# Delta rule in one Trainium2 program: key-query and key-key products merged into one 256-column matmul, decay rows from one 512-column matmul

## Chip, cores and metric

One NeuronCore of one Trainium2 (trn2) chip runs the whole program. The metric is the device time of one execution in microseconds, as the median of several runs; lower is better. TensorE's clock has two levels here, 2.4 and 1.2 GHz, and the profile prints the granted level as 1.00 and 0.50, or a mean between them.

## The reference

The program is four transformer-like layers on an array of shape (8, 512, 128). The change touches only the attention of the last layer, a gated delta rule with 8 heads, key size 128 and value size 32:

```python
def step(state, inp):
    q_t, k_t, v_t, a_t, b_t = inp
    retained = jnp.einsum('bhvk,bhk->bhv', state, k_t)
    rk = retained[..., None] * k_t[:, :, None, :]
    vk = v_t[..., None] * k_t[:, :, None, :]
    state = a4 * (state - b4 * rk) + b4 * vk
    o_t = jnp.einsum('bhvk,bhk->bhv', state, q_t)
    return (state, o_t)
```

Here `a_t = exp(g)` is the decay and `b_t` the write strength. q, k and v come from a projection, a causal convolution of four taps and silu; the output is normalised, gated and projected.

## The kernel before

The recurrence over 512 positions is done in four chunks of 128 positions. Eight heads are split into two groups of four. A *unit* of work is one group of one batch row: its four chunks are inverted and solved, and beside that the data of the next unit (taps, norms, gates, keys) are prepared. The loop body `delta_units` holds two units, called a and b below, and runs 7 times; `delta_first` and `delta_second` come ahead of it, `delta_last` behind it. I write a0 to a3 and b0 to b3 for the four chunk periods of units a and b in the loop body.

Each chunk period has nine turns, 0 to 8, and every engine's program is written out by `in_turn` in the same order of turns. In chunk period i three things go on at once:

- `solve` of chunk i-1 (turn 0 "state": products with the state S; then four small triangular steps; turn 8 "finish": output and new state),
- `make` of chunk i+1 in three parts (turns 0, 3 and 6),
- `invert` of chunk i (32x32 block products, one per turn),

and then the pieces of `prepare` that `pieces(u)` sets for this turn. In some turns there are none; of these, the prediction names turn 6 of a3, b0, b1 and b3 (b0 has only a ScalarE piece there), where TensorE has nothing from `prepare`.

The parts of `make`, with the lines of the kernel before:

- Part 0. TensorE writes the running sum of the decay along the rows into bank 1 (`mk`): four matmuls of 128 columns, one a head (L1725). VectorE subtracts and clips it into `D` (L2013), ScalarE takes the exponential (L1928), POOL masks it with `upto3` (L1893).
- Part 1. TensorE makes the key-query products of four heads in bank 1 (L1733, `kq`); VectorE multiplies them with `D` into `P` (L2018).
- Part 2. TensorE makes the key-key products in the same bank (L1733 again, `kk`), after `P` was read; VectorE scales `D` by `gam` (L2023) and multiplies into `A` (L2026); ScalarE copies A's diagonal blocks (L1932); POOL makes `M` from them (L1898).

A float32 matmul appears in the trace as two records, so four matmuls are "x8". `solve` uses banks 2 and 7 in turn, one for even and one for odd chunks. Its "state" step waits on TensorE for `S` and for the output of the chunk two before (`outs`), then runs L1778; VectorE's side reads the bank at L2059 and L2060, computes `r` (L2062, L2067), copies `W` (L2070), and at turns 7 and 8 makes `zz` and `ze` (L2073, L2076), then `S` (L2087), `o1` (L2088) and `O` (L2090). TensorE's "finish" is L1796 and L1803. The inverse is L1740 on TensorE, L1938 on ScalarE and L2039 with the transpose L2041 on VectorE. POOL also squares q and k for their norms (L1918, waits for ScalarE's silu L1962), copies the input (L1905) and weights the gates (L1910). The taps are L1841, the squares' sums L1849, the norm's second matmul L1817.

## Time and profile before

| | |
|---|---|
| median of 3 runs | 4906.73 us (4898.85 to 4908.08) |
| the profiled execution, its own time | 4906.74 us |
| its span, first to last instruction | 4904.7 us |
| mean granted clock of TensorE over the span | 0.779 |
| TensorE matmul, weight load, VectorE, ScalarE, POOL busy | 81%, 52%, 49%, 31%, 15% |
| delta rule, 2925 to 4790 us of the span | TensorE busy 1707.31 of 1865.00 us |

The profile is of one execution. It gives busy time by engine, strips over 40 slices of the span, groups of instructions by line with the idle time ahead of them, and, for any stretch, the instructions in order of time. Idle time of an engine counts only where the engine sets the pace.

### The profile page before, as it was taken

The numbers are of one execution on the slowest core, as the hardware profiler recorded it, in microseconds if no ns is written. First come the engines' busy times: TensorE is split into PE (matmuls) and PEld (weight loads), VectorE is DVE, ScalarE is ACT, GpSimd is POOL, SyncE is SP. The second block draws the span as 40 slices with busy tenths as digits, with TensorE's granted clock in tenths as the row PEclk, the third lists the DMA queues.
The fourth block names the chain that finished last, engine by engine and source line by source line (L and its number), as shares of the span: only waits on it lengthen the run. The fifth ranks groups of instructions, "written<-read, shape, count | busy, mean of one in ns | idle before, by whom it ended". The sixth has DMA issues, their size and how long they took to land. (4 is left out here: it accounts for less than half of the span.)

```text
span 4904.7 us, 125869 instructions
## 1 busy us (share of the span) xinstructions
PE 3978.9 (81%) x55640; PEld 2529.9 (52%) x55640; DVE 2418.5 (49%) x6071; ACT 1503.3 (31%) x2781; POOL 747.0 (15%) x741
## 2 busy tenths in 40 slices
PE   3557776999858787878787868999898989999985
PEld 1225663444335555555554324666666666666671
DVE  3556775233277777777771112444344443434444
ACT  2443233455422222222212322322232222223223
POOL 1112221000021212111110002211111212111111
PEclk8776667999865556655557979898898889888967
DMA  2000000422000000000000010000000000000000
GB/s 73 0 0 1 0 0 6 64 35 35 15 2 3 3 3 3 3 3 3 3 3 14 0 53 1 2 2 2 2 2 2 2 2 2 2 2 2 2 2 19
DMA packets 18964, 45.89 MB, mean 9 GB/s; under 512 B 4864, under 2 KB 8320, under 8 KB 17408
## 3 DMA queue, kind: packets, MB, share of 16 engines
q1 hardware_dynamic: 18432, 37.95, 3.3%
q8 instruction: 438, 7.18, 0.6%
q14 instruction: 94, 0.77, 0.1%
HBM read 35.71 MB, written 2.23 MB: 8 GB/s over the span
## 5 line engine op out<-in xcount | busy, mean ns | idle before, releaser
L1841 PE MATMUL ps<-d_hp,d_w_qk 128*128 128x512 f32 x1024 | 520.0, 632 | 8.0 <-ACT d_QK L1962 8.0
L1031 PE MATMUL ps<-g_Q,g_K 32*32 32x32 f32 (+1 forms) x12288 | 275.7, 246 | 28.5 <-issue 12.9
L1841 PEld LDWEIGHTS ps<-d_hp,d_w_qk 128*128 128x128 f32 x1024 | 179.3, 194 | 226.2 <-issue 201.0
L1031 PEld LDWEIGHTS ps<-g_Q,g_K 32*32 32x32 f32 x12288 | 238.0, 134 | 73.7 <-PE ps L1031 39.3
L852 PE MATMUL ps<-ex_hs,w_c_fc 128*128 128x512 f32 x512 | 232.7, 598 | 20.1 <-DVE ex_hs L818 20.1
L1938 ACT ACTIVATE d_F<-ps 128x128 f32<-128x128 f32 x256 | 70.8, 277 | 520.1 <-PE ps L1740 519.7
L863 PE MATMUL ps<-ex_r,w_c_proj 128*128 128x512 f32 x512 | 230.0, 592 | 0.0
L1063 PE MATMUL ps<-g_S,g_V 32*64 32x32 f32 x4096 | 160.6, 287 | 79.7 <-DVE g_H L1239 60.5
L826 DVE TENSOR_TENSOR ex_r<-ex_r 128x512 f32<-128x512 f32 x128 | 88.5, 692 | 277.2 <-ACT ex_r L840 277.2
L840 ACT ACTIVATE ex_r<-ps 128x512 f32<-128x512 f32 x256 | 151.5, 592 | 236.4 <-PE ps L852 236.3
L2070 DVE COPY d_W<-ps 32x128 f32<-32x128 f32 x256 | 73.0, 285 | 277.6 <-PE ps L1790 275.5
L1898 POOL TENSOR_TENSOR d_M<-d_A,w_joins 128x128 f32<-128x128 f32 (+1 forms) x128 | 112.0, 896 | 588.0 <-ACT d_A L1932 588.0
L1918 POOL TENSOR_TENSOR d_sq<-d_QK 128x512 f32<-128x512 f32 x128 | 133.1, 1042 | 402.4 <-ACT d_QK L1962 353.2
L1063 PEld LDWEIGHTS ps<-g_S,g_V 32*64 32x64 f32 x4096 | 127.4, 203 | 128.9 <-DVE g_H L1239 69.1
L2067 DVE TENSOR_TENSOR d_r<-d_r,ps 32x128 f32<-32x128 f32 x192 | 55.0, 287 | 264.0 <-PE ps L1783 247.9
L1047 PE MATMUL ps<-g_V,g_KT 32*32 32x64 f32 x4096 | 154.2, 286 | 25.0 <-issue 5.3
L1928 ACT ACTIVATE d_D<-d_D 128x512 f32<-128x512 f32 x64 | 40.3, 629 | 434.3 <-DVE d_D L2013 434.2
L852 PEld LDWEIGHTS ps<-ex_hs,w_c_fc 128*128 128x128 f32 x512 | 98.1, 192 | 144.1 <-issue 123.4
L1778 PE MATMUL ps<-d_S,d_QK 128*128 128x32 f32 x768 | 137.1, 345 | 36.2 <-issue 32.5
L1733 PE MATMUL ps<-d_QK 128*128 128x128 f32 x1024 | 162.0, 306 | 0.8 <-DVE d_P L2018 0.8
L1740 PE MATMUL ps<-d_X,d_M 32*32 32x32 f32 x8192 | 129.7, 199 | 38.4 <-DVE d_X L2036 24.5
L1893 POOL TENSOR_TENSOR d_D<-d_D,w_upto 128x512 f32<-128x512 f32 x64 | 85.5, 1335 | 492.4 <-ACT d_D L1928 492.4
(464 smaller groups left out, 8263.6 us busy)
## 6 DMA issues: line engine op xcount, KB each, us to landing
ex_root<-gate_rows SPq DMA_DIRECT2D x8, 2048.0 KB, 15.4
d_QK<-in_conv_qk_dram SPq DMA_DIRECT2D x2, 2048.0 KB, 7.4
X<-in_x_dram SPq DMA_DIRECT2D x1, 2048.0 KB, 11.4
w_c_fc<-in_c_fc_dram SPq DMA_DIRECT2D x1, 2048.0 KB, 7.7
w_c_proj<-in_c_proj_dram SPq DMA_DIRECT2D x1, 2048.0 KB, 12.1
out_dram<-X SPq DMA_DIRECT2D x1, 2048.0 KB, 6.3
w_wmod<-in_wmod_dram SPq DMA_DIRECT2D x1, 1536.0 KB, 6.8
w_w<-in_w_dram SPq DMA_DIRECT2D x2, 768.0 KB, 5.3
```

The costliest lines, as they stand in the source:

```text
L840: e.activation(r[:, n % 2, f], hidden(f), ACT.Relu).then_inc(act.steps, act.did(f"r{n}{f}"))
L852: e.matmul(hidden(f), k.w["c_fc"][:, n % E, ts(f, C)], hs[:, n % 3], start=True, stop=True).then_inc(pe.steps, pe.did(f"u{n}{f}"))
L863: e.matmul(total(b), k.w["c_proj"][:, x, f, :], r[:, n % 2, f], start=(x == 0 and f == 0), stop=(x == E - 1 and f == F - 1)).then_inc(pe.s ...
L1031: ins = e.matmul(later(scored, n_), keys_, queries(n_, planes, r, 4 * i + j), start=(turn_ == 0 and part == 0 and n_ != 1), stop=(part == ...
L1047: ins = e.matmul(P[2 * odd + 1][ts(h4, 32), 256 + j * 64:320 + j * 64], KT[rows, (KR, KI)[part], i, ts(h4, 32)], V[rows, i, 4 * sg + h4, ( ...
L1063: ins = e.matmul(P[4 + bank][ts(second, 64), t], V[rows, i, 4 * sg + h4, (slice(32, 96), slice(0, 64))[part]], S[rows, i % 2, h4, part, :] ...
L1733: ins = e.matmul(mk[:, ts(h, C)], QK[:, 1, H, t], QK[:, part - 1, H, t], start=True, stop=True)
L1740: ins = e.matmul(inv[rows, h], stationary[rows, h], moving[rows, h], start=True, stop=True, tile_position=(32 * j, 32 * j))
L1778: ins = e.matmul(b[:, half * 128 + 32 * h:half * 128 + 32 * h + 32], QK[:, what, H, ts(c, C)], S[:, H], start=True, stop=True)
L1841: ins = e.matmul(b, w_qk[:, j, c, ts(H, C)], hp[:, j:j + T], start=(j == 0), stop=(j == TAPS - 1))
L1898: e.tensor_tensor(M[:, a, levels], A32[:, a].unsqueeze(1).to_broadcast([C, many, 4, 32]), k.w["joins"][:, levels].unsqueeze(2).to_broadcas ...
L1918: e.tensor_tensor(squares(x), qk, qk, ALU.mult).then_inc(pool.steps, pool.did(f"{tag}sq{x}"))
```

## The change

The two groups of products of a chunk become one: for each head one matmul with the key as stationary side and query and key together as 256 moving columns. Their results need two banks: heads 0 and 1 in bank 1, heads 2 and 3 in bank 7. So `solve` has bank 2 alone, and its "state" step waits for the output of the chunk just before. The decay's rows come from one matmul of 512 columns with `ones3` as stationary side, over a product of `upto3` and `g` that POOL writes into `D` (new part 3 of `make`). VectorE reads the two banks in two instructions for `P` and two for `A`, each of 256 columns.

```diff
-        bank = lambda i: P[(2, 7)[i % 2]]
+        pair = [P[x].rearrange("p (h w x) -> p w h x", h=2, w=2) for x in (1, 7)]
+        bank = lambda i: P[2]
         MAKE = {0: 0, 3: 1, 6: 2}
+        MAKE_SECOND = {0: 3, 2: 0, 4: 1, 6: 2}
+        EARLY = NI - 1
...
+                            if t == 3 * NI - 1:
+                                make(u, NT, 3)
...
-                            if turn in MAKE and (i + 1 < NT or u["next"]):
-                                make(u, i + 1, MAKE[turn])
+                            parts = MAKE if i else MAKE_SECOND
+                            if turn in parts and (i + 1 < NT or u["next"]):
+                                make(u, i + 1, parts[turn])
                             invert(u, i, step, l)
                             for piece in at[NI * i + turn]:
                                 prepare(u, *piece)
+                            if turn == EARLY and (i + 2 < NT or i + 2 == NT and u["next"]):
+                                make(u, i + 2, 3)
... tensor engine
-                            for h in range(4):
-                                ins = e.matmul(mk[:, ts(h, C)], q["g"][:, c, 4 * g + h:4 * g + h + 1].to_broadcast([C, C]), k.w["upto3"][:], start=True, stop=True)
-                            ins.then_inc(pe.steps, pe.did(f"gb{n}"))
+                            e.wait_ge(pool.steps, pool.at(f"u{n}"))
+                            e.matmul(mk, k.w["ones3"][:], f2(D[:, g]), start=True, stop=True).then_inc(pe.steps, pe.did(f"gb{n}"))
...
-                            e.wait_ge(dve.steps, dve.at((f"d{n}", f"P{n}")[part - 1]))
+                            e.wait_ge(dve.steps, dve.at(f"d{n}"))
                             for h in range(4):
                                 H = 4 * g + h
-                                ins = e.matmul(mk[:, ts(h, C)], QK[:, 1, H, t], QK[:, part - 1, H, t], start=True, stop=True)
-                            ins.then_inc(pe.steps, pe.did((f"kq{n}", f"kk{n}")[part - 1]))
+                                ins = e.matmul(pair[h // 2][:, :, h % 2], QK[:, 1, H, t], QK[:, :, H, t], start=True, stop=True)
+                            ins.then_inc(pe.steps, pe.did(f"kk{n}"))
...
-                            if c % 2 in outs:
-                                e.wait_ge(dve.steps, dve.at(f"out{outs[c % 2]}"))
-                            outs[c % 2] = n
+                            if outs:
+                                e.wait_ge(dve.steps, dve.at(f"out{outs[-1]}"))
+                            outs.append(n)
... gpsimd
+                        if part == 3:
+                            if i == NT:
+                                e.wait_ge(dve.steps, dve.at(u["tag"] + "g"))
+                            if made:
+                                e.wait_ge(dve.steps, dve.at(f"A{made[-1]}"))
+                            made.append(n)
+                            e.tensor_tensor(D[:, g], k.w["upto3"][:].unsqueeze(1).to_broadcast([C, 4, C]),
+                                            q["g"][:, c, 4 * g:4 * g + 4].unsqueeze(2).to_broadcast([C, 4, C]), ALU.mult).then_inc(pool.steps, pool.did(f"u{n}"))
... vector engine
-                            e.tensor_tensor(Pm[:, a], v4(mk), D[:, g], ALU.mult).then_inc(dve.steps, dve.did(f"P{n}"))
+                            for x in range(2):
+                                e.tensor_tensor(Pm[:, a, ts(x, 2)], pair[x][:, 0], D[:, g, ts(x, 2)], ALU.mult).then_inc(dve.steps, dve.did(f"P{n}"))
...
-                            e.wait_ge(pe.steps, pe.at(f"kk{n}"))
                             e.wait_ge(dve.steps, dve.at(f"dg{n}"))
-                            e.tensor_tensor(A[:, a], v4(mk), D[:, g], ALU.mult).then_inc(dve.steps, dve.did(f"A{n}"))
+                            for x in range(2):
+                                e.tensor_tensor(A[:, a, ts(x, 2)], pair[x][:, 1], D[:, g, ts(x, 2)], ALU.mult).then_inc(dve.steps, dve.did(f"A{n}"))
```

The first place is TensorE in a0, from the second state-solving step to the start of a1. Before, in program order:

```order
L1790 MATMUL ps<-d_r,d_Y 32x32 x4
L1733 MATMUL ps<-d_QK 128x128 x4
L1740 MATMUL ps<-d_X,d_M 32x32 x16
L1817 MATMUL ps<-d_sq,w_mean 128x512
L1783 MATMUL ps<-d_W,d_A 32x32 x4
L1740 MATMUL ps<-d_F,d_Y 32x32 x16
L1868 MATMUL ps<-w_ident,d_QK 128x128 x4
L1790 MATMUL ps<-d_r,d_Y 32x32 x4
L1740 MATMUL ps<-d_X,d_M 32x32 x16
L1783 MATMUL ps<-d_W,d_A 32x32 x4
L1733 MATMUL ps<-d_QK 128x128 x4
L1740 MATMUL ps<-d_F,d_Y 32x32 x16
```

And of the change, the same stretch (its lines carry other numbers: L1795 is L1790 of before, L1745 is L1740, L1818 or L1822 the norm, L1788 is L1783, L1873 is L1868):

```order
L1795 MATMUL ps<-d_r,d_Y 32x32 x4
L1745 MATMUL ps<-d_X,d_M 32x32 x16
L1822 MATMUL ps<-d_sq,w_mean 128x512
L1788 MATMUL ps<-d_W,d_A 32x32 x4
L1738 MATMUL ps<-d_QK 128x256 x4
L1745 MATMUL ps<-d_F,d_Y 32x32 x16
L1873 MATMUL ps<-w_ident,d_QK 128x128 x4
L1795 MATMUL ps<-d_r,d_Y 32x32 x4
L1745 MATMUL ps<-d_X,d_M 32x32 x16
L1788 MATMUL ps<-d_W,d_A 32x32 x4
L1745 MATMUL ps<-d_F,d_Y 32x32 x16
```

The products of turn 3 are now at turn 4 (only in the first chunk period of a unit; else they stay at turn 3) and twice as wide, and nothing stands any more between L1783's and L1740's successors at turn 6.

The second place is POOL in a0 and the start of a1. Before, from the loop's start:

```order
L1893 TENSOR_TENSOR d_D<-d_D,w_upto 128x512
L1905 ISA
L1905 COPY d_xb<-X 128x512
L1898 TENSOR_TENSOR d_M<-d_A,w_joins 128x128
L1898 TENSOR_TENSOR d_M<-d_A,w_joins 128x512
L1910 TENSOR_TENSOR d_values_gates<-d_values_gates,w_o_norm_w 128x4x128
L1918 TENSOR_TENSOR d_sq<-d_QK 128x512
L1893 TENSOR_TENSOR d_D<-d_D,w_upto 128x512
```

And of the change:

```order
L1904 TENSOR_TENSOR d_D<-w_upto,d_g 128x512
L1920 ISA
L1920 COPY d_xb<-X 128x512
L1908 TENSOR_TENSOR d_D<-d_D,w_upto 128x512
L1913 TENSOR_TENSOR d_M<-d_A,w_joins 128x128
L1913 TENSOR_TENSOR d_M<-d_A,w_joins 128x512
L1925 TENSOR_TENSOR d_values_gates<-d_values_gates,w_o_norm_w 128x4x128
L1933 TENSOR_TENSOR d_sq<-d_QK 128x512
L1904 TENSOR_TENSOR d_D<-w_upto,d_g 128x512
L1908 TENSOR_TENSOR d_D<-d_D,w_upto 128x512
```

L1904 is the new product, once at the very start and once for chunk 2; the second stands behind the first square of q and k (L1933, before L1918), and TensorE's decay matmul of a1 (L1731) waits for it.

The third place is ScalarE at the start of unit a. Before:

```order
L1928 ACTIVATE d_D<-d_D 128x512
L1938 ACTIVATE d_F<-ps 128x128
L1948 ACTIVATE d_sq<-ps 128x512
L1958 ACT_TABLE_LOAD
L1958 ACTIVATE d_values_gates<-ps 128x2x128 x3
L1938 ACTIVATE d_F<-ps 128x128
```

And of the change:

```order
L1953 ACTIVATE d_F<-ps 128x128
L1963 ACTIVATE d_sq<-ps 128x512
L1973 ACT_TABLE_LOAD
L1973 ACTIVATE d_values_gates<-ps 128x2x128 x2
L1943 ACT_TABLE_LOAD
L1943 ACTIVATE d_D<-d_D 128x512
L1973 ACT_TABLE_LOAD
L1973 ACTIVATE d_values_gates<-ps 128x2x128
L1953 ACTIVATE d_F<-ps 128x128
```

The exponential of `D` now stands between silus, with a table load on either side of it.

## Rows read from the trace of the kernel before

**Rows 1.** The page: busy time, share of the span and count, by engine.

```profile
PE 3978.9 (81%) x55640; PEld 2529.9 (52%) x55640; DVE 2418.5 (49%) x6071; ACT 1503.3 (31%) x2781; POOL 747.0 (15%) x741
```

**Rows 2.** Windows: busy time by engine in one loop iteration and one calm stretch.

```profile
core 0: us, PE busy (x) PEld busy (x) DVE busy (x) ACT busy (x) POOL busy (x), PEclk, DMA share, GB/s
3319.00:3551.00 232.00, 213.96 (x3220) 147.65 (x3221) 95.30 (x295) 64.64 (x150) 44.17 (x43) 0.88 0.01 2
3398.00:3430.30 32.30, 30.51 (x500) 25.87 (x501) 13.80 (x48) 7.32 (x21) 5.66 (x6) 0.75 0.01 2
```

**Rows 3.** Timeline (start, duration, engine, line) of TensorE: two taps, then the next group.

```profile
3349.61 1.96 PE L1841 MATMUL ps<-d_hp,d_w_qk 128*128 128x512 f32 x4
3351.50 0.43 PE L1790 MATMUL ps<-d_r,d_Y 32*32 32x32 f32 x8
```

**Rows 4.** Timeline of turn 6 and 7 in b1, TensorE and VectorE.

```profile
3484.96 1.16 PE L1733 MATMUL ps<-d_QK 128*128 128x128 f32 x8
3485.39 0.69 DVE L2023 TENSOR_TENSOR d_D<-d_D,d_gam 128x512 f32<-128x512 f32 x1
...
3486.05 0.45 PE L1740 MATMUL ps<-d_F,d_Y 32*32 32x32 f32 x32
3486.19 0.69 DVE L2026 TENSOR_TENSOR d_A<-ps,d_D 128x512 f32<-128x512 f32 x1
...
3486.34 0.41 PE L1790 MATMUL ps<-d_r,d_Y 32*32 32x32 f32 x8
3486.79 0.28 DVE L2039 TENSOR_TENSOR d_X<-d_X,ps 128x128 f32<-128x128 f32 x1
...
3487.12 0.45 PE L1740 MATMUL ps<-d_X,d_M 32*32 32x32 f32 x32 [0.37 <-DVE d_X L2039]
```

**Rows 5.** Timeline of the key-query products in a3, at the lower clock.

```profile
3414.09 2.08 PE L1733 MATMUL ps<-d_QK 128*128 128x128 f32 x8
```

**Rows 6.** Timeline from turn 7 of a0 to turn 0 of a1, all engines.

```profile
3342.95 1.68 POOL L1898 TENSOR_TENSOR d_M<-d_A,w_joins 128x128 f32<-128x128 f32 x2 [14.70 <-ACT d_A L1932]
...
3343.61 1.17 DVE L2073 TENSOR_TENSOR d_zz<-d_W,d_gam 128x128 f32<-128x128 f32 x1
...
3344.70 1.75 DVE L2108 TENSOR_TENSOR d_values_gates<-d_values_gates,d_kn 128x512 f32<-128x512 f32 x1
...
3348.36 1.05 PE L1725 MATMUL ps<-w_upto,d_g 128*128 128x128 f32 x8
...
3349.42 0.60 ACT L1962 ACTIVATE d_QK<-ps 128x512 f32<-128x512 f32 x1
...
3350.09 1.04 POOL L1918 TENSOR_TENSOR d_sq<-d_QK 128x512 f32<-128x512 f32 x1 [4.19 <-ACT d_QK L1962]
```

**Rows 7.** The same place in the last of the 7 iterations, TensorE and POOL.

```profile
4497.82 1.05 PE L1725 MATMUL ps<-w_upto,d_g 128*128 128x128 f32 x8
```

```profile
4499.55 1.04 POOL L1918 TENSOR_TENSOR d_sq<-d_QK 128x512 f32<-128x512 f32 x1 [4.19 <-ACT d_QK L1962]
```

**Rows 8.** Timeline of the end of b2: POOL, VectorE, TensorE.

```profile
3516.29 1.67 POOL L1898 TENSOR_TENSOR d_M<-d_A,w_joins 128x128 f32<-128x128 f32 x2 [5.68 <-ACT d_A L1932]
...
3517.05 1.06 DVE L2073 TENSOR_TENSOR d_zz<-d_W,d_gam 128x128 f32<-128x128 f32 x1
...
3518.15 1.01 DVE L2076 TENSOR_TENSOR d_ze<-d_zz,d_end 128x128 f32<-128x128 f32 x1
...
3519.21 0.52 PE L1796 MATMUL ps<-d_zz,d_P 128*128 128x32 f32 x3 [2.27 <-DVE d_ze L2076]
```

**Rows 9.** Windows around two idle places of TensorE: columns as in rows 2.

```profile
3516.40:3519.80 3.40, 1.13 (x46) 1.01 (x44) 2.37 (x3) 2.05 (x3) 2.61 (x3) 1.00 0.02 5
3519.80:3530.00 10.20, 10.20 (x75) 8.92 (x74) 3.02 (x13) 0.00 (x0) 0.00 (x0) 0.50 0.00 0
3461.80:3465.20 3.40, 1.91 (x50) 1.67 (x49) 2.28 (x7) 0.64 (x2) 0.48 (x1) 1.00 0.00 0
3465.20:3468.60 3.40, 3.40 (x4) 0.89 (x4) 2.25 (x8) 1.03 (x6) 1.17 (x1) 0.50 0.00 0
```

**Rows 10.** Timeline at the end of unit a.

```profile
3425.46 1.06 PE L1778 MATMUL ps<-d_S,d_QK 128*128 128x32 f32 x4
3425.50 0.29 DVE L2090 TENSOR_TENSOR d_O<-d_o,d_qn 128x128 f32<-128x128 f32 x1
```

**Rows 11.** The page's groups: POOL's masking of `D`.

```profile
L1893 POOL TENSOR_TENSOR d_D<-d_D,w_upto 128x512 f32<-128x512 f32 x64 | 85.5, 1335 | 492.4 <-ACT d_D L1928 492.4
```

15 lines of the change are left out of this document (7 added, 8 removed).

## Prediction

> **What bounds the kernel now.** I read the page's busy shares first: TensorE is busy 81% of the span, VectorE 49%, POOL 15% [rows 1]. Then the windows by stage: in one iteration of the delta loop TensorE works 213.96 of 232.00 us at a mean clock of 0.88 [rows 2]. So here TensorE's queue sets the pace; a microsecond counts when it lengthens that queue, opens a gap in it, or turns the clock down. The chain that ended last lies in the last layers and says nothing of this stage, so I read the timeline of one iteration engine by engine instead. The reader should see two kinds of place: turns in which TensorE has taps or sums behind the small steps and never waits, and turns without them, where it waits for VectorE (0.37 us in [rows 4]). An iteration comes 7 times; I cost one iteration and multiply. The profiled execution took 4906.74 us with a span of 4904.7, the same as the median of the runs to 0.01 us.
>
> **The products.** Four heads of 128 columns take 1.09 us from their start to the next group's (3484.96 to 3486.05, [rows 4]). Two taps of 512 columns take 1.89 us (3349.61 to 3351.50, [rows 3]), 0.945 each, against 0.27 for one head. No row has 256 columns. Between the two, 0.27 + (0.945 - 0.27)/3 = 0.495 a head, so 1.98 us for four; since the 0.27 holds the start of a group I take 1.95. The bounds are 1.09 (columns free) and 2.18 (nothing saved). The two old groups took 2.18, so a chunk saves 0.23 us of TensorE's work. The decay's rows went from four matmuls of 128 columns to one of 512: 0.945 against about 0.98 to 1.09, nothing.
>
> The Trainium skill ("TensorE: Matmul & The Clock Gate", section "Wait — 56ns, not 53.3ns?") gives a fixed cost of about 2.5 ns a matmul beside its columns. By that page eight records fewer are an estimated 0.02 us a chunk in place of 0.23, which would add 0.2 us to each chunk's term; the rows above show more than that, since a group's start is in them.
>
> **Where the products stand.** This matters more than their sum. All of the work is now at turn 3 (4 in a0 and b0), 0.86 us longer than before, and 1.09 us are gone from turn 6. In [rows 4], turn 6 without a piece, VectorE goes from `D` times `gam` (3485.39, 0.69) to `A` (3486.19, 0.69) to the subtraction of X (3486.79 to 3487.07), and TensorE's next step waits for that. With the key-key products gone, `A` could start 0.1 us earlier and is two instructions in place of one, which I bound by one more start, about 0.1: the subtraction ends when it did. TensorE comes there 1.09 us earlier and waits 1.09 us longer. These periods (a3, b0, b1, b3) keep the 0.86 us of turn 3 and get nothing back. In a3 and b3 the products run at the lower clock, 2.08 in place of 1.16 us [rows 5], so 0.86 becomes 1.54. Together 2 x 0.86 + 2 x 1.54 = **+4.8 us**. a1 has sums and a tap at turn 6 and saves its 0.23: **-0.2**. In a2 TensorE waits at "finish" anyway, so of 1.09 I give back a third: **+0.5**.
>
> In b2 "finish" waits 2.27 us for `ze`: `zz` takes 1.06 us beside POOL's M and `ze` 1.01 beside a square [rows 8], where a free one takes about the 0.28 of the X subtraction [rows 4]. If `W` comes up to 1.09 us earlier, `zz` starts at 3515.96, ahead of M at 3516.29, and at least 1.1 us of the wait go; if `ze` slips in too, 2.7 go. Net of 0.86 that is -0.2 to -1.8; I take **-0.5**.
>
> **POOL's new product.** It is priced by the masking of the same size, 1.3 us [rows 11]. In most periods POOL is done with it before TensorE asks. At a1 it isn't: it stands behind the first square, which waits for ScalarE's silu (3349.42) and ends at 3351.13; the product would end at 3352.4, while TensorE's decay matmul started at 3348.36 [rows 6]: 4.0 us late. In the last iteration it is the same, 4499.55 + 1.04 + 1.3 against 4497.82 [rows 7], and all seven lie at 4.0. Queued behind the waiting matmul are the gates' sums and the next tap; nothing else can go on. The lower bound: turn 6 is shorter, so `zz` might start ahead of M and not take 1.17, nor `values` 1.75 beside POOL [rows 6]; that brings the silu up to 2.9 us forward and leaves 1.1. I take **+3.1**, nearer to the row. The rule behind the 1.17 and 1.75 is in the Trainium skill ("SBUF — State Buffer", section "Who interferes with whom"): a VectorE instruction with two SBUF inputs is shut out while a GpSimd instruction reads SBUF; by that rule, the trace agrees.
>
> **The clock.** Where TensorE idled 2.27 us of 3.40 the next 10.20 us ran at 0.50; where it idled 1.49 the next 3.40 did [rows 9]. So the wait at a1 (over 3 us for TensorE) should be followed by at least 3.4 us at half speed, in which the work of 1.7 us is lost: **+1.7** (0 to 5.1).
>
> **Small ones.** With one bank for `solve`, "state" waits for `O`. Everywhere but at the end of unit a there is work between; there it started at 3425.46 and `O` ended at 3425.79 [rows 10]: **+0.4**. The table loads around the exponential (two more in a0) fall while ScalarE is mostly free; in b0 the silu that frees a bank comes later: **+0.3**, were that cover gone 1.3 each. Weight loads fall from eight to four heads' worth and lie under matmuls.
>
> **Sum.** 4.8 - 0.2 + 0.5 - 0.5 + 3.1 + 1.7 + 0.4 + 0.3 = 10.1 us an iteration, 71 us for seven. Outside the loop are eight more periods, in which turn 6 is mostly bare: 8 x 0.6 = 5. That is +76 on a span of 4904.7, and 4906.7 + 76 = **4983 us**.
>
> **Rivals.**
> - *The product isn't late* (18%). If the earlier `zz` pulls the silu forward, the term falls to 1.1 and the clock stays up: 10.1 - 2.0 - 1.7 = 6.4 an iteration, 4957 us. For it speaks that 1.09 us earlier is enough in [rows 6] to pass M; against it, that the norm ahead of it sets this point too.
> - *Faster through the clock* (10%). Around a3 and around b3 the clock has a mean of 0.75 over 32.30 us [rows 2]: half of the time at half speed, so 8 us of work are lost at each, 113 us in all. A denser, wider stream of products could hold the higher level. It decides from 76/113, two thirds of that, on; were all of it won, the time would be 4870. Against it: turn 6 becomes emptier at the same place.
> - *Nothing comes of it* (6%): VectorE and TensorE regain in the busy periods what the bare turns lose, since all the waits there are under 0.4 us; 4905.
> - *The clock falls at the bare turns too* (8%): their wait grows to 1.46 us, like the 1.49 of [rows 9]. Four times 1.7 us and seven iterations are 48 more: 5031.
> - The forecast, slower as summed: 58%, its own range 4960 to 5015.
>
> **How the numbers follow.** The range 4925 to 5030 takes in the first rival, the lower bounds of the products and of the wait (4.0 to 1.1), and the last rival's edge; outside are the two that end at or below 4905. Two tenths of a per cent, about 10 us, is what a measurement can tell from no change. Faster 0.10, same 0.06, slower 0.84.
>
> **What would show it.** In the trace of the change: the group of 256 columns at 1.95 us start to next start; an idle of some 1.4 us ahead of the first inverse product of turn 7 in b1, released by VectorE's X; ahead of the decay matmul of a1 an idle of 2 to 4 us released by POOL, and a window at 0.50 behind it; an iteration of 242 us in place of 232. The prediction is wrong if the iteration's mean clock rises above 0.90, if the wait for POOL's product is missing, or if turn 6 turns out to be covered.

## The result, and the profile of the change

The change made the kernel slower: 5026.84 us (median of 4 runs, 5022.06 to 5038.62) against 4906.83 us for the kernel before on the same chip, a ratio of 1.0252 with a 95% interval of 1.0231 to 1.0273. The forecast said 4983 us, with 4960 to 5015 as its own range and 4925 to 5030 as the range over all rivals. Direction and mechanism of most terms hold, the size does not: 120 us in place of 76. The profiled execution took 5038.62 us, span 5036.9 us. It is the slowest of the four, 12 us above the median, so what is read from its trace per iteration of the loop is somewhat high, by some 1.7 us if all of the 12 us lie there (12 / 7).

The page's busy time of the changed kernel, which answers to [rows 1]:

```profile
PE 4052.0 (80%) x54744; PEld 2497.7 (50%) x54744; DVE 2421.7 (48%) x6199; ACT 1521.4 (30%) x2795; POOL 812.9 (16%) x805
```

896 TensorE records fewer, yet 73 us more busy. The windows of the changed kernel: the loop iteration that answers to the first line of [rows 2], then the wait at a1 and the stretch behind it.

```profile
core 0: us, PE busy (x) PEld busy (x) DVE busy (x) ACT busy (x) POOL busy (x), PEclk, DMA share, GB/s
3338.08:3585.72 247.64, 221.07 (x3105) 140.67 (x3105) 97.01 (x311) 67.11 (x152) 52.46 (x51) 0.85 0.01 2
3368.00:3371.10 3.10, 0.04 (x1) 0.07 (x1) 0.00 (x0) 2.08 (x3) 2.04 (x2) 1.00 0.00 0
3371.10:3376.00 4.90, 4.90 (x12) 2.20 (x13) 3.41 (x9) 0.63 (x1) 1.65 (x1) 0.65 0.02 3
```

The mean clock of the iteration went from 0.88 to 0.85: that is where the part of the loss that the forecast lacks will turn out to be. First the places that the prediction named. The timeline of the changed kernel at a1, ScalarE, POOL and TensorE:

```profile
3368.21 0.60 ACT L1977 ACTIVATE d_QK<-ps 128x512 f32<-128x512 f32 x1
...
3368.88 1.04 POOL L1933 TENSOR_TENSOR d_sq<-d_QK 128x512 f32<-128x512 f32 x1 [4.20 <-ACT d_QK L1977]
3369.88 1.04 POOL L1904 TENSOR_TENSOR d_D<-w_upto,d_g 128x512 f32<-128x512 f32 x1
...
3371.06 1.10 PE L1731 MATMUL ps<-d_D,w_ones 128*128 128x512 f32 x2 [4.02 <-POOL d_D L1904]
...
3372.57 3.44 PE L1846 MATMUL ps<-d_hp,d_w_qk 128*128 128x512 f32 x4
```

POOL's product is queued behind the square, which waits for the silu; TensorE idles 4.02 us for it, and the next two taps take 3.44 us in place of the 1.98 that a pair takes at the full clock. This iteration is the exception: in the six others the same wait is 2.46 to 2.53 us. Turns 3, 6 and 7 of b1, TensorE and VectorE, which answer to [rows 4]:

```profile
3505.60 1.99 PE L1738 MATMUL ps<-d_QK 128*128 128x256 f32 x8
3507.53 0.45 PE L1745 MATMUL ps<-d_X,d_M 32*32 32x32 f32 x32
...
3519.24 0.43 PE L1795 MATMUL ps<-d_r,d_Y 32*32 32x32 f32 x8
...
3520.62 0.28 DVE L2055 TENSOR_TENSOR d_X<-d_X,ps 128x128 f32<-128x128 f32 x1
...
3520.95 0.45 PE L1745 MATMUL ps<-d_X,d_M 32*32 32x32 f32 x32 [1.27 <-DVE d_X L2055]
```

The wide group takes 1.93 us to the next start, and at the bare turn 6 TensorE waits 1.27 us for VectorE, where it waited 0.37.

TensorE's waits over the seven iterations, the changed kernel first, then the kernel before. Columns: engine and line that waits, what ended it, us in total, times, the longest.

```profile
PE ps L1783 <- issue: 32.7, 6, 6.9
PE ps L1745 <- DVE d_X L2055: 31.4, 28, 1.3
PE ps L1801 <- DVE d_ze L2092: 29.5, 31, 2.3
PE ps L1745 <- DVE d_X L2052: 20.5, 16, 1.5
PE ps L1731 <- POOL d_D L1904: 19.0, 7, 4.0
```

```profile
PE ps L1778 <- issue: 32.5, 6, 5.6
PE ps L1796 <- DVE d_ze L2076: 25.1, 27, 2.3
PE ps L1740 <- DVE d_X L2036: 20.6, 15, 1.5
...
PE ps L1740 <- DVE d_X L2039: 9.8, 27, 0.4
```

"issue" is time for which the profile shows no releaser; it stands at the head of the loop body and is the same in both. The bare turns cost 21.6 us more (31.4 - 9.8), POOL's product 19.0, `ze` 4.4: 45 us of new waiting in the loop, while the loop is 121 us longer. The windows over the seven iterations, kernel before and change:

```profile
3092.79:4689.76 1596.97, 1477.31 (x22512) 1011.98 (x22513) 667.30 (x2066) 452.68 (x1051) 309.13 (x301) 0.89 0.01 2
```

```profile
3093.78:4811.65 1717.87, 1542.60 (x21729) 981.91 (x21729) 670.37 (x2178) 471.01 (x1065) 367.25 (x358) 0.85 0.01 2
```

TensorE is idle for 175.3 us in place of 119.7, so 56 of the 121 us are idle time; the other 65 are time in which it is busy, though it has less to do.

To see it by place I matched the steps of `solve` on TensorE in both traces and took the mean length of each chunk period over the seven iterations. "half" is the time of an iteration in which TensorE's clock is granted at 0.50. All kernels below are in it; the numbers are differences to the kernel before in us, which has an iteration of 228.1 us.

```
kernel (label)      iter.    a0    a1    a2    a3    b0    b1    b2    b3   half
before              228.1     0     0     0     0     0     0     0     0   49.7
the change         +17.3   +4.9  +0.3  +2.5  +3.6  +5.2  +1.2  -2.1  +1.6   72.3
e1_ahead           +13.3   +1.8  +0.2  +2.3  +2.9  +5.1  +1.7  -1.9  +1.3   70.3
e2_split           +11.7   +5.2  -0.2  +0.7  +0.8  +3.4  -0.1  +1.8  +0.1   66.7
e3_products         +7.9   +4.4  +0.2  +1.4  +3.3  -0.3  -0.5  -2.6  +2.0   57.1
e4_rows             +9.3   +5.4  -0.2  +0.3  -0.4  +2.9  -0.9  +1.7  +0.5   63.8
e5_split_ahead      +5.5   -0.8  +1.0   0.0  +1.1  +3.3  -0.5  +1.7  -0.3   58.6
e6_onebank          +2.1   -0.1   0.0  +0.1  +0.5  +1.2  -1.1  +0.3  +1.2   53.2
e7_fill            +17.7   +4.9  +0.5  +4.2  +0.8  +3.4  +3.2  -0.3  +1.1   62.9
e8_before_fill      +4.0   +0.5   0.0  +0.1  +1.8  -0.7  +0.5  +0.2  +1.6   45.3
e9_halves           +2.0   -0.1  +0.1   0.0  +0.4  -0.6  -0.1  +0.6  +1.8   54.6
e10_late            +3.5   -0.8  +0.1   0.0  -0.8  +3.9  +0.1  +1.7  -0.5   57.5
e11_mixed           +2.9   +0.5  +0.2  +2.2   0.0  -0.5   0.0  +0.3  +0.2   51.6
e12_one_period      +3.1   -0.1   0.0  +1.7  +0.7  +0.7   0.0  +0.1  -0.1   53.2
e13_mixed_b         +2.6   +1.3   0.0  +0.2  -0.6  +3.8  -0.5  -1.2  -0.4   55.6
e14_b2_alone        +0.1   +2.4   0.0   0.0  -0.4  -0.7  +0.2  -1.9  +0.6   50.7
```

A period runs here from the first step of its `solve` on TensorE to the next one's; a1 and b1 have no products with the state and so begin a turn later, which puts the wait for POOL's product into a0. A row of this table is one execution. How much one carries shows the kernel before itself: its seven iterations, which hold the same instructions, last 221.3 to 232.7 us with 37.0 to 62.0 us at half speed. Differences under some 2 us an iteration in one row are not read here unless several rows repeat them.

In the change, half-speed time rose by 22.6 us an iteration. If all work done at half speed took twice its time, 11.3 us of the 17.3 would be the clock's, and 6.0 the balance of waits and work. This is an estimate from above: a group of products takes 2.08 us in place of 1.16 at the lower clock [rows 5], a group of small ones 0.65 in place of 0.45, and a little of the half-speed time is idle. It fits the windows: 7.9 us more idle an iteration (55.6 / 7), less 1.8 for the eight times 0.23 us of work that the wide products were to save.

### The profile page after: what moved, and what is told of

Same layout as the page of the kernel before. It is cut to its first block and busy times, and to the rows that moved or that the text cites. A ratio compares the mean times of both kernels' runs of the same rounds, so it can differ in the third digit from the quotient of the medians.

```text
span 5036.9 us, 124267 instructions
## 1 busy us (share of the span) xinstructions
PE 4052.0 (80%) x54744; PEld 2497.7 (50%) x54744; DVE 2421.7 (48%) x6199; ACT 1521.4 (30%) x2795; POOL 812.9 (16%) x805
## 5 line engine op out<-in xcount | busy, mean ns | idle before, releaser
L1846 PE MATMUL ps<-d_hp,d_w_qk 128*128 128x512 f32 x1024 | 550.3, 664 | 7.0 <-ACT d_QK L1977 7.0
L1933 POOL TENSOR_TENSOR d_sq<-d_QK 128x512 f32<-128x512 f32 x128 | 133.3, 1044 | 355.5 <-ACT d_QK L1977 298.1
L1745 PE MATMUL ps<-d_X,d_M 32*32 32x32 f32 x8192 | 133.6, 201 | 65.8 <-DVE d_X L2055 39.4
L1783 PE MATMUL ps<-d_S,d_QK 128*128 128x32 f32 x768 | 148.0, 362 | 39.8 <-issue 32.7
L1783 PEld LDWEIGHTS ps<-d_S,d_QK 128*128 128x128 f32 x768 | 145.3, 290 | 53.9 <-issue 41.1
L987 POOL TENSOR_TENSOR g_tmp<-g_rs 128x512 f32<-128x512 f32 x16 | 24.7, 1543 | 868.9 <-ACT g_rs L1172 868.9
## 6 DMA issues: line engine op xcount, KB each, us to landing
w_c_proj<-in_c_proj_dram SPq DMA_DIRECT2D x1, 2048.0 KB, 12.2
```

The source lines that it names most:

```text
L1745: ins = e.matmul(inv[rows, h], stationary[rows, h], moving[rows, h], start=True, stop=True, tile_position=(32 * j, 32 * j))
L1783: ins = e.matmul(b[:, half * 128 + 32 * h:half * 128 + 32 * h + 32], QK[:, what, H, ts(c, C)], S[:, H], start=True, stop=True)
L1846: ins = e.matmul(b, w_qk[:, j, c, ts(H, C)], hp[:, j:j + T], start=(j == 0), stop=(j == TAPS - 1))
L1933: e.tensor_tensor(squares(x), qk, qk, ALU.mult).then_inc(pool.steps, pool.did(f"{tag}sq{x}"))
```

## The experiments

Each states the edit, what was expected, the time and its ratio to the kernel before, and what follows; the row by period is in the table above.

### The two halves of the change apart

**e3_products**: the change without its decay rows; `make` part 0 is again four matmuls at turn 0.

```diff
-                            parts = MAKE if i else MAKE_SECOND
+                            parts = MAKE
...
-                            if turn == EARLY and (i + 2 < NT or i + 2 == NT and u["next"]):
-                                make(u, i + 2, 3)
...
-                            e.wait_ge(pool.steps, pool.at(f"u{n}"))
-                            e.matmul(mk, k.w["ones3"][:], f2(D[:, g]), start=True, stop=True).then_inc(pe.steps, pe.did(f"gb{n}"))
+                            for h in range(4):
+                                ins = e.matmul(mk[:, ts(h, C)], q["g"][:, c, 4 * g + h:4 * g + h + 1].to_broadcast([C, C]), k.w["upto3"][:], start=True, stop=True)
+                            ins.then_inc(pe.steps, pe.did(f"gb{n}"))
...
```

> The merged products alone: two banks, one bank for the solve, 256 columns at turn 3, VectorE's halves; the decay's rows are again four matmuls of 128 columns without POOL's product, and all periods have the old turns 0, 3 and 6. Theory: keeps the seven periods' loss and adds the 0.9 of turn 3 in a0, without the wait of a0: 4907 + 7 x 12.4 + 10 = about 5000 us. Rival (the rows and the late order of the first period are what costs): under 4950 us.

Measured 4968.34 us, 1.0149 (1.0122 to 1.0177): between the theory and the rival. The bare turns are all there (28 waits for VectorE's X, 35.6 us in the loop), yet half-speed time rises by 7.4 us an iteration only, and in b0 and b1 it is 6.5 and 0.0 us where the kernel before has 9.0 and 2.9. What is long is a0 (+4.4), with 15.7 us at half speed in place of 7.2, though this kernel has no late product there; why was not tried.

**e4_rows**: the kernel before with POOL's product, the matmul of 512 columns and `MAKE_SECOND`, nothing else.

```diff
+        MAKE_SECOND = {0: 3, 2: 0, 4: 1, 6: 2}
...
-                            if turn in MAKE and (i + 1 < NT or u["next"]):
-                                make(u, i + 1, MAKE[turn])
+                            parts = MAKE if i else MAKE_SECOND
+                            if turn in parts and (i + 1 < NT or u["next"]):
+                                make(u, i + 1, parts[turn])
...
+                            if turn == EARLY and (i + 2 < NT or i + 2 == NT and u["next"]):
+                                make(u, i + 2, 3)
...
-                            for h in range(4):
-                                ins = e.matmul(mk[:, ts(h, C)], q["g"][:, c, 4 * g + h:4 * g + h + 1].to_broadcast([C, C]), k.w["upto3"][:], start=True, stop=True)
-                            ins.then_inc(pe.steps, pe.did(f"gb{n}"))
+                            e.wait_ge(pool.steps, pool.at(f"u{n}"))
+                            e.matmul(mk, k.w["ones3"][:], f2(D[:, g]), start=True, stop=True).then_inc(pe.steps, pe.did(f"gb{n}"))
...
```

> The decay's rows alone: the kernel before with POOL's product, the 512-column matmul and the new turns of the first period; products, banks and waits of the solve as before. Theory: only the late product at a1 with its stretch at half speed, 7 x 4.9 = 34 us, so about 4941 us, with turn 6 covered. Rival (the new order of a unit's first period costs in b0 too): 4960 us or more.

Measured 4973.11 us, 1.0156 (1.0137 to 1.0175): the rival. My terms for the halves were 5.0 us an iteration (4.8 - 0.2 + 0.5 - 0.5 + 0.4) and 5.1 (3.1 + 1.7 + 0.3); measured are 7.9 and 9.3. In the profiled loops they add up to 17.2 us an iteration where the change has 17.3, but that is chance. By place they do not add: a0 would be 9.8 and is 4.9, b0 2.6 and is 5.2, b1 -1.4 and is +1.2. Nor do they by the whole time: 1.49 and 1.56% make 3.05%, the change has 2.52%, some 26 us less. So the halves interact. One way is on record: the wait for POOL's product is 3.87 to 3.89 us in all seven iterations of e4, and 2.5 in six of seven in the change.

### POOL's product and the order of turns

**e1_ahead**: POOL's product is issued ahead of the pieces of turn 8, so ahead of the square.

```diff
+                            if turn == EARLY and (i + 2 < NT or i + 2 == NT and u["next"]):
+                                make(u, i + 2, 3)
                             for piece in at[NI * i + turn]:
                                 prepare(u, *piece)
-                            if turn == EARLY and (i + 2 < NT or i + 2 == NT and u["next"]):
-                                make(u, i + 2, 3)
```

> The changed kernel with one move: at turn 8 POOL's new product is issued ahead of the turn's pieces, so it no longer stands behind the first square. Theory (the two parts of the loss are separate: the product that comes late at a1, and the products' new place, which leaves turn 6 bare and brings the clock down): the 4.9 us that period a0 gained go almost wholly, 7 x 4.5 = 32 us, so about 4995 us. Rival (a0 is long for other reasons, such as the table loads or the single bank of the solve): within 5 us of the changed kernel, 5022 to 5030.

Measured 5015.28 us, 1.0242 (1.0213 to 1.0272), between the theory and the rival. The wait at a1 is gone. Timeline of e1, POOL and TensorE at a1:

```profile
3365.47 1.08 POOL L1904 TENSOR_TENSOR d_D<-w_upto,d_g 128x512 f32<-128x512 f32 x1
...
3369.46 1.02 PE L1731 MATMUL ps<-d_D,w_ones 128*128 128x512 f32 x2
```

a0 falls from +4.9 to +1.8: here the late product was worth 3.1 us an iteration. Hardly any of it is the clock's, for a0 keeps 11.8 of its 12.2 us at half speed without the wait. Between e2 and e5 below the same move is worth 6.0 (a0 from +5.2 to -0.8). My 4.8 lies between. In e2 the wait itself is longer (3.9 us), and there half-speed time in a0 does fall with it, from 11.5 to 6.7 us. The whole-time ratios of e1 and of the change overlap; on the time alone this experiment would be inconclusive, the trace decides.

**e10_late**: the kernel before with nothing but the parts of the first period of a unit moved.

```diff
+        MAKE_SECOND = {2: 0, 4: 1, 6: 2}
...
-                            if turn in MAKE and (i + 1 < NT or u["next"]):
-                                make(u, i + 1, MAKE[turn])
+                            parts = MAKE if i else MAKE_SECOND
+                            if turn in parts and (i + 1 < NT or u["next"]):
+                                make(u, i + 1, parts[turn])
```

> The kernel before, with the parts of make in the first chunk period of a unit at turns 2, 4 and 6 in place of 0, 3 and 6, and nothing else. Theory: the later order alone costs b0 what it costs in all kernels with the new rows (2.9 us an iteration, two of them at the half clock) and a0 nothing: 4920 to 4930 us. Rival: that loss belongs to POOL's product and the matmul of 512 columns, and the order is free: 4903 to 4912.

Measured 4931.38 us, 1.0055 (1.0034 to 1.0076), as the theory said. Only the order was edited, but ScalarE pays for it with two more table loads an iteration (17 in place of 15), since the exponential of `D` now stands between silus. The order costs 3.9 us in b0 and 3.5 an iteration, of the 9.3 us of e4. How it does, by the steps of `solve` on TensorE as means of seven iterations: turn 0 gives back 0.6 us. From turn 1 to 3 it is 2.2 us more, of which 1.1 is the decay's group and the rest is at half speed. From turn 3 to 5 it is 0.6 more, and that is a wait: in every iteration of e10 and of the change TensorE waits 0.66 us in b0 for the silu of the values, which now stands behind the exponential and a table load; the kernel before has no such wait. From the taps of turn 7 on it is 1.7 more. ScalarE and TensorE in b0 of e10:

```profile
3451.02 0.63 ACT L1930 ACTIVATE d_D<-d_D 128x512 f32<-128x512 f32 x1 [6.05 <-DVE d_D L2015]
3451.66 1.28 ACT L1960 ACT_TABLE_LOAD   x1
3452.96 0.66 ACT L1960 ACTIVATE d_values_gates<-ps 128x256 f32<-128x256 f32 x2
...
3453.40 1.16 PE L1832 MATMUL ps<-d_w_v,d_hp 128*128 128x128 f32 x8 [0.66 <-ACT d_values_gates L1960]
```

And the clock: b0 has 15.5 us at half speed in place of 9.0. The timeline of TensorE at turn 7 of b0 and its windows, first of the kernel before, then of e10:

```profile
3454.79 0.45 PE L1740 MATMUL ps<-d_X,d_M 32*32 32x32 f32 x32 [0.38 <-DVE d_X L2039]
...
3456.83 1.98 PE L1841 MATMUL ps<-d_hp,d_w_qk 128*128 128x512 f32 x4 [1.00 <-ACT d_QK L1962]
```

```profile
3424.13:3456.83 32.70, 31.33 (x430) 25.06 (x429) 10.97 (x39) 7.29 (x22) 3.28 (x5) 0.79 0.01 2
3456.83:3459.60 2.77, 2.77 (x16) 1.77 (x19) 0.18 (x1) 1.89 (x3) 2.77 (x3) 1.00 0.03 6
```

```profile
3465.09 0.45 PE L1742 MATMUL ps<-d_X,d_M 32*32 32x32 f32 x32 [0.37 <-DVE d_X L2041]
...
3467.13 3.27 PE L1843 MATMUL ps<-d_hp,d_w_qk 128*128 128x512 f32 x4 [0.99 <-ACT d_QK L1964]
```

```profile
3434.43:3467.13 32.70, 30.67 (x426) 23.84 (x426) 10.88 (x39) 7.18 (x22) 3.18 (x4) 0.80 0.01 2
3467.13:3470.00 2.87, 2.87 (x4) 1.28 (x5) 0.18 (x1) 1.89 (x3) 2.87 (x3) 0.60 0.02 6
```

The same two waits, 0.38 and 1.00 against 0.37 and 0.99 us, ahead of the same pair of taps; one runs at the full clock and takes 1.98 us, the other takes 3.27. In the 32.70 us ahead TensorE was busy for 31.33 us in one and 30.67 in the other; the difference is the one wait of 0.66 us, some 14 us earlier. It does not settle the clock either: behind this tap the kernel before has no half-speed time in any of the seven iterations, e10 and the change 3.4 us in each of them, and e4, which has all three waits of e10 (0.66, 0.37 and 1.00 us), in two of seven.

### The wide products taken apart

**e2_split**: the change with its two banks kept, but key-query products again at turn 3 and key-key at turn 6.

```diff
-                                ins = e.matmul(pair[h // 2][:, :, h % 2], QK[:, 1, H, t], QK[:, :, H, t], start=True, stop=True)
+                                ins = e.matmul(pair[h // 2][:, 0, h % 2], QK[:, 1, H, t], QK[:, 0, H, t], start=True, stop=True)
+                            ins.then_inc(pe.steps, pe.did(f"kq{n}"))
+                        elif part == 2:
+                            e.wait_ge(dve.steps, dve.at(f"P{n}"))
+                            for h in range(4):
+                                H = 4 * g + h
+                                ins = e.matmul(pair[h // 2][:, 1, h % 2], QK[:, 1, H, t], QK[:, 1, H, t], start=True, stop=True)
...
```

> The changed kernel with the 256-column products split again: key-query at turn 3 (4 in the first period) and key-key at turn 6, each 128 columns a head, still in the two banks and with VectorE's halves; POOL's product and the 512-column matmul stay. TensorE has 0.2 us more work a chunk. Theory (place): turn 6 is covered again, the seven other periods give back what they lost, 12.4 x 7 = 87 us, so about 4940 us, and TensorE's half-speed time in an iteration falls from 72 us back towards 50. Rival (the two halves, the single bank or the late O cause the loss, or it comes from the POOL product in every period): at least 4990 us.

Measured 4991.86 us, 1.0191 (1.0171 to 1.0211): the rival. Turn 6 covered again gives back 0.6%, not the 87 us of the theory. **e5_split_ahead** has both moves, e1's and e2's.

> Both moves on the changed kernel: POOL's product ahead of the turn's pieces, and the products split again over turns 3 and 6. What is left of the change is the 512-column matmul over POOL's product, the order of a unit's first period, the single bank and VectorE's halves. The split alone gave 35 us and the product ahead 12. Theory (they add, and the trace of the product ahead showed 22 us in a0): 4992 less 12 to 22, 4970 to 4980 us. Rival (once turn 6 is covered a0's wait is all that the rows cost): about 4940 us.

Measured 4948.42 us, 1.0075 (1.0059 to 1.0092), again the rival: the theory that the two moves add is refuted. Each move alone gains 0.1 and 0.6%, both together 1.8%. What is left in e5, +3.3 in b0 and +1.7 in b2, is what e10 has there (+3.9 and +1.7). e2 itself shows a2 back at +0.7, but b2 has lost its gain.

**e6_onebank**: the kernel before with bank 2 alone for `solve` and the wait for the output just before. **e9_halves**: the kernel before with `P` and `A` in two instructions each.

```diff
-        bank = lambda i: P[(2, 7)[i % 2]]
+        bank = lambda i: P[2]
...
-                            if c % 2 in outs:
-                                e.wait_ge(dve.steps, dve.at(f"out{outs[c % 2]}"))
-                            outs[c % 2] = n
+                            if outs:
+                                e.wait_ge(dve.steps, dve.at(f"out{outs[-1]}"))
+                            outs.append(n)
```

```diff
-                            e.tensor_tensor(Pm[:, a], v4(mk), D[:, g], ALU.mult).then_inc(dve.steps, dve.did(f"P{n}"))
+                            for x in range(2):
+                                e.tensor_tensor(Pm[:, a, ts(x, 2)], v4(mk)[:, ts(x, 2)], D[:, g, ts(x, 2)], ALU.mult).then_inc(dve.steps, dve.did(f"P{n}"))
... the same for A
```

> The kernel before with one bank in place of two for the solve, and the wait for the output of the chunk just before; nothing else. The split kernel is 19 us slower than the decay's rows alone, and this is one of the two things that it has more (VectorE's halves are the other). Theory (a late O costs only where no piece stands between, once or twice an iteration, 0.4 us each): 3 to 6 us, 4906 to 4909 against 4902.5. Rival (it carries the 19 us): about 4920.

> The kernel before, with VectorE's P and A each in two instructions of 256 columns. If a second start is all that it costs (some 0.1 us ahead of the subtraction of X in the four bare turns 6, 28 times), the time is 4907 to 4911 us. If what the two halves add to the bare turns tips the clock as the whole change did, 4915 to 4930.

Measured 4922.95 us, 1.0024 (1.0011 to 1.0037), and 4917.03 us, 1.0029 (1.0014 to 1.0044). Both are real and small, 12 and 14 us by the ratios, where the prediction had 3 us (0.4 x 7) for the bank and nothing for the halves. In both the time is nearer to the rival than to the theory. In e9 TensorE's step behind the X subtraction comes 0.06 us later at most bare turns 6, where 0.1 was expected; the rest is in b3's half-speed time (21.5 us against 16.3), which one execution does not settle.

### Is it the clock? Useless work in the holes

**e7_fill** is the change, **e8_before_fill** the kernel before, each with four matmuls of 128 columns into a bank at bare turns; their result is used by nothing. There are four such groups an iteration in both, at the same places: turn 6 of a3, b0, b1 and b3.

```diff
+            if u["next"] and u["g"] is not None:
+                for t in ((33,) if new else (6, 15, 33)):
+                    at[t] += [("fill", t)]
...
+                        elif what == "fill":
+                            emptied(e, u, "fill", x)
+                            for h in range(4):
+                                e.matmul(ring_bank(u, "fill", x)[:, ts(h, C)], k.w["ident"][:], k.w["center"][:], start=True, stop=True)
```

The filler is not free of side effects: `ring_bank` gives it one of the three banks that taps, values and keys take in turn, so the pieces behind it get other banks and wait for them at other times. In e7 the output's projection in b1 now waits 1.31 us for a bank that a silu has to empty; in the change it doesn't wait.

> The changed kernel with useless work: in the bare turns 6 (periods b0, b1, a3 and b3) TensorE gets four more matmuls of 128 columns, about 1.1 us, into a bank of the ring that is free; nobody reads them, outputs are unchanged. Theory (the emptied turn 6 costs mostly through the clock, TensorE idles 0.7 to 1.3 us there and then runs at half speed): the added work fits into the idle time, the half-speed time of an iteration falls from 72 us towards 60 and the time falls by 20 to 50 us, to 4980 to 5005. Rival (the clock is not caused by these gaps, only TensorE's work counts): 7 x 4 x 0.2 to 1.1 us more, 5030 to 5055.

> The control: the same useless matmuls in the kernel before, where the key-key products cover turn 6 and TensorE idles only 0.4 us there. Theory: about 0.7 us more at each of 28 places, partly paid back where a stretch at half speed goes: 4905 to 4925 us. Rival (any more work at this place helps the clock as much as in the changed kernel): 4860 to 4890 us.

Measured 5035.6 us, 1.0246 (1.0225 to 1.0267), and 4949.13 us, 1.0099 (1.0082 to 1.0115). The theory for the change, 20 to 50 us faster, has failed, and the time is the rival's. The filler's groups of 1.1 us cost nothing there: the waits for X fall from 1.3 to 0.3 us and half-speed time from 72.3 to 62.9 us an iteration, by 8.0 in a3, 4.4 in b0 and 3.6 in b3, three of the four places of the filler, though it rises by 1.0 in the fourth and by some 4 each in a2 and b2. That fits holes at the bare turns that feed the lower clock in this kernel; e3, with the same holes, shows that they need not. What the clock gives is used up: the waits for POOL's product rise from 19.0 to 26.3 us in the loop and those for a bank that ScalarE's silu has yet to empty from 7.0 to 20.3, so filling the holes with useless work was no remedy here. In the kernel before, whose holes are 0.4 us, the filler costs 42 to 49 us, more than both the theory (up to 20 us) and the rival (a gain) had. TensorE's waits over the seven iterations of e8:

```profile
PE ps L1801 <- DVE d_ze L2085: 40.7, 28, 2.3
...
PE ps L1877 <- ACT d_QK L1971: 6.7, 7, 1.0
PE ps L1890 <- ACT d_QK L1971: 4.8, 7, 0.7
```

The waits for X at the bare turns are gone (9.8 us), but those for `ze` rise from 25.1 to 40.7 us: the filler delays `W`, so that in a3 and b3 `zz` and `ze` now run beside POOL's M, and `ze` takes 1.24 and 1.10 us in place of 0.29. So part of the filler's price is a collision of the kind that the next experiments show. Half-speed time is 45.3 against 49.7, within the spread.

### The place where the wide products gain

In the change, in e1 and in e3, b2 got faster (-1.9 to -2.6). Is this a gain of its own? **e11_mixed** and **e12_one_period** put wide products into the kernel before for chunks 1 and 3, or chunk 3 alone, of one unit, and keep two banks for `solve`. For these chunks `P` and `A` are in two instructions each, and "state" also waits for the last `A` made.

```diff
-        bank = lambda i: P[(2, 7)[i % 2]]
+        pair = [P[x].rearrange("p (h w x) -> p w h x", h=2, w=2) for x in (1, 7)]
+        bank = lambda i: P[(7, 2)[i % 2]]
+        both = lambda g, c: g == 1 and c in (1, 3)
...
```

> The kernel before, with the merged products (256 columns, banks 1 and 7) only for the chunks made in b0 and b2, and the solve banks so chosen that no other wait arises. Theory: the products at turn 3 pay where VectorE's zz then passes POOL's M (b2, 2.6 us an iteration where only the products were merged) and cost nothing in b0: 4887 to 4897 us. Rival: the gain in b2 was the clock's, given back in b3: 4903 to 4920.

> The kernel before, with the merged products for the chunk made in b2 alone, solve banks as in the mixed kernel. Theory: 2.6 us an iteration less in b2 and nothing elsewhere, 4888 to 4895 us. Rival, that the gain is given back in b3: 4903 to 4915.

Measured 4929.25 us, 1.0051 (1.0032 to 1.007), and 4931.32 us, 1.0053 (1.0036 to 1.007). These times say nothing of the expectations, for I had taken the wrong unit: in the loop g is 1 for unit a, so the wide products were made in a0 and a2. The miss was worth having, since it shows a2, where the change loses 2.5 us, by itself: +1.7 and +2.2. **e13_mixed_b** and **e14_b2_alone** have `g == 0`, so b0 and b2, and b2 alone.

> As the mixed kernel, but with the merged products really for the chunks made in b0 and b2; in the mixed kernel they fell to a0 and a2, because the group number of unit b in the loop is 0. Theory: 0 in b0, and the 2.6 us an iteration in b2 that the products-alone kernel showed: 4885 to 4895 us. Rival: the gain in b2 is the clock's or is given back in b3: 4903 to 4920.

> The merged products for the chunk made in b2 alone. Theory: the wait of finish for ze in b2 goes, 2 to 2.6 us an iteration, nothing elsewhere: 4885 to 4895 us. Rival, given back in b3: 4903 to 4915.

Measured 4917.74 us, 1.0029 (1.0016 to 1.0041), in the rival's range, and 4895.19 us, 0.9984 (0.9971 to 0.9996), at the edge of the theory's. The mechanism is one and the same in a2 and b2, with opposite signs. Timeline of POOL, VectorE and TensorE at the end of a2, kernel before, then e12:

```profile
3398.81 1.68 POOL L1898 TENSOR_TENSOR d_M<-d_A,w_joins 128x128 f32<-128x128 f32 x2 [6.25 <-ACT d_A L1932]
...
3400.62 0.29 DVE L2073 TENSOR_TENSOR d_zz<-d_W,d_gam 128x128 f32<-128x128 f32 x1
...
3401.29 1.08 PE L1796 MATMUL ps<-d_zz,d_P 128*128 128x32 f32 x8 [0.79 <-DVE d_ze L2076]
```

```profile
3404.41 1.68 POOL L1905 TENSOR_TENSOR d_M<-d_A,w_joins 128x128 f32<-128x128 f32 x2 [6.24 <-ACT d_A L1939]
...
3405.14 1.09 DVE L2089 TENSOR_TENSOR d_zz<-d_W,d_gam 128x128 f32<-128x128 f32 x1
...
3407.33 1.08 PE L1803 MATMUL ps<-d_zz,d_P 128*128 128x32 f32 x8 [2.31 <-DVE d_ze L2092]
```

And at the end of b2 in e14, which answers to [rows 8]:

```profile
3505.29 0.29 DVE L2089 TENSOR_TENSOR d_zz<-d_W,d_gam 128x128 f32<-128x128 f32 x1
3505.61 1.73 POOL L1905 TENSOR_TENSOR d_M<-d_A,w_joins 128x128 f32<-128x128 f32 x2 [5.67 <-ACT d_A L1939]
3505.62 0.60 DVE L2092 TENSOR_TENSOR d_ze<-d_zz,d_end 128x128 f32<-128x128 f32 x1
...
3506.27 1.08 PE L1803 MATMUL ps<-d_zz,d_P 128*128 128x32 f32 x8 [1.09 <-DVE d_ze L2092]
```

`zz` now starts 1.09 us earlier beside M. In a2 it was after M (1.81 us behind its start) and is now inside it (0.73 behind), so it takes 1.09 us, `ze` after it runs into the square, and "finish" waits 2.31 us in place of 0.79. In b2 it was inside M and is now ahead of it. By the rule of the Trainium skill ("SBUF — State Buffer", section "Who interferes with whom"), who is issued first decides which of VectorE and GpSimd is shut out; these rows agree for `zz`: it takes 0.29 us when it starts before M and 1.09 when it starts 0.73 us after it. They do not for `ze` in b2: it starts 0.01 us behind M, which takes 1.73 us for its two instructions, and takes 0.60 us, so it is held up by a part of M only.

e13's b0 costs 3.8 us, where e3's, with the same wide products there, costs nothing: 15.6 us at half speed against 6.5. e14 is a little faster than the kernel before, some 8 us by its ratio, though its interval nearly touches 1 and its loop is no shorter: b2 gives 1.9 us an iteration, and a new stall at the loop's start takes 2.4. Timeline of TensorE there:

```profile
3305.92 0.42 PE L1785 MATMUL ps<-d_S,d_QK 128*128 128x32 f32 x1 [5.07 <-issue]
3309.46 3.20 PE L1785 MATMUL ps<-d_S,d_QK 128*128 128x32 f32 x15 [3.13 <-issue]
```

All other kernels but e13 have one idle stretch of 5 to 6 us there (6.9 once), and nothing of 0.6 us or more behind it; e14 has a second of 2.6 to 3.1 us in six iterations, e13 one of 0.8 to 1.3. The profile names no releaser. Its cause was not tried. Of the 14 us by which e14's profiled execution reaches the loop earlier, 8 lie ahead of the first step of `solve`, where the wide products can't matter, so part of the gain may be the spread of executions.

## Why the prediction was wrong

By period of an iteration, the prediction's terms against the change's row (the late `O` counted in a3, the table loads in b0):

| | forecast | measured |
|---|---|---|
| a0: product late 3.1, clock after it 1.7 | +4.8 | +4.9 |
| a1 | -0.2 | +0.3 |
| a2: a third of 1.09 | +0.5 | +2.5 |
| a3: 1.54, late `O` 0.4 | +1.9 | +3.6 |
| b0: 0.86, tables 0.3 | +1.2 | +5.2 |
| b1: 0.86 | +0.9 | +1.2 |
| b2 | -0.5 | -2.1 |
| b3: 1.54 | +1.5 | +1.6 |
| sum | +10.1 | +17.3 |

**Right.** The wide group at 1.93 us from start to next start (forecast 1.95); the wait of over 1 us at the bare turns by VectorE's X (28 waits, 9.8 to 31.4 us in all, 1.27 us in b1 where 1.46 was forecast); the wait for POOL's product and what it is queued behind; b2 faster because `zz` passes M. TensorE was the bound, and the saved work was lost in waits.

**Right by luck.** a0 meets its forecast to 0.1 us by other parts. The wait for the product is 2.7 us in the mean and not 3.1 (2.5 in six of seven iterations, where the text had all seven at 4.0). Half-speed time in a0 rises by 5.0 us, but e1, which has no such wait, keeps nearly all of it, and e3, which has no late product at all, has a0 at +4.4.

**Wrong, and the step that failed: "The clock".** The prediction gave the clock one term, +1.7 us behind the wait at a1 (beside the 1.54 for two periods that were at half speed already). Measured are 22.6 us more at half speed an iteration, up to 11.3 us of lost work. The rest of the sum, 8.4 us, stands against some 6.0 measured. So the error of 7.2 us is this term, 9.6 too small, less 2.4 that the others were too high.

A rival had named the clock: "The clock falls at the bare turns too", with 8% and 5031 us, close to what came out. Its number is right in good part by luck. It wants half speed at a3, b0, b1 and b3. In the change a3 and b0 did gain (16.4 us against 10.4, 16.6 against 9.0), b1 and b3 hardly (3.9 against 2.9, 17.9 against 16.3). And e3, which has all of the bare turns' waits, gained 7.4 us an iteration at half speed and lost some in b0 and b1, while e4, where these waits are as before, gained 14.1. b0's gain comes with the order of the first period: e10 has 15.5 us there. So the term that failed is the clock's as a whole; the place that the rival gave it is not what the runs show.

**Two smaller steps failed by place.** In b0 the forecast had 0.86 for the products, nothing for the decay's rows at turn 2 in place of turn 0, and 0.3 for the table loads, where "the silu that frees a bank comes later". e10 shows that the order of b0 alone costs 3.9 us with its clock, most of the missing 4: turn 0 gives back 0.6 us for the 1.1 that turn 2 gets, the late silu costs 0.66, and the rest is the clock. And in a2 "of 1.09 I give back a third" overlooked that the same 1.09 us that bring `zz` ahead of M in b2 bring it into M in a2: the rows for it lie in the same trace, at 3398.81 and 3400.62. In b2 the same mechanism gave 2.1 in place of 0.5, more than the bound of 1.8 that the prediction had for it, so the two nearly cancel (+2.0, -1.6).

**Small:** the one bank (1.0024) and VectorE's halves (1.0029), some 12 and 14 us each. They were taken as 3 us and nothing.

**Open.** What decides whether a wait of this size is followed by half speed. The rows show the same wait with both outcomes; no run here separates the causes. Also open are how the two halves interact beyond the shorter wait for POOL's product, and why a0 is long in e3. How much of the clock's 11.3 us each new wait is worth is therefore shown only as sums of whole kernels (half-speed time: order alone +7.8 us an iteration, halves +4.9, one bank +3.5, products 7.4, rows 14.1, all 22.6), and single numbers of these lie near the spread of one execution. The +9.2 us from the loop's end to the last "finish" in the change, against +5 forecast for all outside the loop, was not taken apart.

## What to carry to other kernels

Work that stands in a turn without other cover is itself the cover: moving it to a fuller turn is a cost even when it gets smaller, so ask at both ends of the move what the queue will wait for. In a stream with many short waits a new one can cost twice, by its length and by the clock that follows; where a trace shows half speed after waits of the size that a change creates, the clock belongs into the sum with a wide range, and not only among the rivals. When an instruction moves between others of its engine, ask what it does to them: here an exponential between silus brought table loads and a wait of 0.66 us on another engine. Two experiments whose effects add up in total can still differ in every place, so compare them by place before calling them independent. And when work on one engine starts a microsecond earlier, look in each period for what it now runs beside, since the same shift can leave a collision in one and enter it in the next.
